# Message stage of a graph network: counts turned as bf16 in runs of eight blocks, one pass for the bias row, TensorE's steps written out

## What is computed

```python
# layer 0: relational convolution
Hb = jnp.einsum('ni,bio->bno', h, V)                  # 4 bases
m = sum_b w_comp[etype][:, b] * Hb[b][src]; m = m * norm
agg = jax.ops.segment_sum(m, dst)
hn = jax.nn.relu(agg + h @ loop_w + bias)
y = hn @ ffn_w.T + ffn_b + h                          # then layer norm with ln_g, ln_b
# layer 1: two transformer convolutions, 2 heads, over the same edges
alpha = jnp.sum(q[dst] * k[src], axis=-1) / np.sqrt(C)
ex = jnp.exp(alpha - segment_max(alpha)[dst])
out = segment_sum(v[src] * ex / segment_sum(ex)[dst]) + x @ Ws + bs
```

## Time and profile before

| what | before |
|---|---|
| median of 3 runs | 2248.89 us |
| the profiled execution, its own time | 2249.5 us |
| its span | 2247.5 us |
| mean granted TensorE clock | 0.981 |
| busy: TensorE, its weight loads | 94%, 76% |
| busy: VectorE, ScalarE, GpSimd | 71%, 57%, 37% |

### The profile page before, as it was taken

One profiled execution on the slowest core, in us unless ns is written; L12 is line 12 of the kernel. 1 busy time (PEld: TensorE's weight loads), 2 busy tenths in 40 slices (PEclk: granted clock), 3 DMA queues, 4 the chain that ended last, 5 costly groups with the idle time before them and its releaser, 6 DMA issues. The chain is left out here.

```text
span 2247.5 us, 55086 instructions
## 1 busy us (share of the span) xinstructions
PE 2104.2 (94%) x19640; PEld 1707.9 (76%) x19640; DVE 1590.5 (71%) x4061; ACT 1291.7 (57%) x2303; POOL 821.2 (37%) x1091
## 2 busy tenths in 40 slices
PE   1299999999999999999997999999999999999998
PEld 1288888898888888888985677777776677777776
DVE  1458887888888888878873666666664666666765
ACT  1156666665666666666663555556564455565555
POOL 0766776777677667767710000000000000000000
PEclk9599999999999999999998999999999999999999
DMA  4001111111111111111112222222221122222220
GB/s 122 14 31 45 42 46 51 44 45 52 47 38 46 51 48 41 46 51 44 43 40 100 87 78 72 80 85 85 85 85 48 71 94 92 92 92 92 92 92 7
DMA packets 52538, 141.57 MB, mean 63 GB/s; under 512 B 9261, under 2 KB 43755, under 8 KB 45855
## 3 DMA queue, kind: packets, MB, share of 16 engines
q1 hardware_dynamic: 49804, 129.55, 16.3%
q0 software_dynamic: 2576, 9.68, 1.5%
HBM read 93.95 MB, written 45.27 MB: 62 GB/s over the span
## 5 line engine op out<-in xcount | busy, mean ns | idle before, releaser
L778 PE MATMUL ps<-matrixT,x_rows 125*128 125x256 f32 (+1 forms) x2500 | 582.7, 384 | 2.9 <-ACT aggT L864 2.1
L778 PEld LDWEIGHTS ps<-matrixT,x_rows 125*128 125x128 f32 x2500 | 461.4, 191 | 70.9 <-issue 3.3
L845 ACT COPY matrixT<-ps 125x500 f32<-125x500 f32 (+2 forms) x800 | 395.8, 583 | 201.5 <-PE ps L766 197.3
L1468 ACT COPY weightsT_l<-ps 125x500 f32<-125x500 f32 (+1 forms) x450 | 233.8, 542 | 369.2 <-PE ps L1389 369.2
L766 PE MATMUL ps<-high_weights,low_onehot 64*125 64x125 f32 x6300 | 403.8, 279 | 23.2 <-issue 11.3
L1546 DVE CUSTOM_DVE_ANT_0 scores_l<-ps,bias_rows_l 125x500 f32<-125x500 f32 (+1 forms) x700 | 396.8, 619 | 35.3 <-issue 33.7
L766 PEld LDWEIGHTS ps<-high_weights,low_onehot 64*125 64x125 f32 x6300 | 366.2, 189 | 54.0 <-issue 37.2
L1389 PEld LDWEIGHTS ps<-eye,scores_l 125*125 125x125 f32 x2500 | 301.1, 189 | 115.6 <-issue 97.2
L1389 PE MATMUL ps<-eye,scores_l 125*125 125x125 f32 x2500 | 364.2, 286 | 4.8 <-ACT scores_l L1450 3.4
L1554 DVE COPY weightsT_l<-ps 125x500 f32<-125x500 f32 (+1 forms) x250 | 150.0, 600 | 267.3 <-PE ps L1389 264.9
L1450 ACT ACTIVATE scores_l<-scores_l,neg_max_l 125x1500 f32<-125x1500 f32 x200 | 320.9, 1605 | 20.5 <-DVE neg_max_l L1583 20.4
(11 more groups left out here) (154 smaller groups left out, 1864.5 us busy)
## 6 DMA issues: line engine op xcount, KB each, us to landing
bias_rows_l<-bias SPq DMA_DIRECT2D x50, 1562.5 KB, 6.7
bias<-bias SPq DMA_DIRECT2D x150, 250.0 KB
edges<-rec POOLq DMA_DIRECT2D x1, 2014.2 KB, 11.8
x_rows<-in_x SPq DMA_DIRECT2D x1, 1562.5 KB
bias<-bias SPq DMA_DIRECT2D x25, 62.5 KB
x<-x_rows SPq DMA_DIRECT2D x25, 62.5 KB
x_rows_l<-x SPq DMA_DIRECT2D x25, 62.5 KB
out<-rows_l SPq DMA_DIRECT2D x25, 62.5 KB
```

The lines of the kernel that those rows point to most:

```text
L778: last = nc.tensor.matmul(psG[:, BASES * SPLIT * side:BASES * (SPLIT * side + SIDE[side])], x[:, h, :], MT[side][:, 0:SIDE[side], BASES * ...
L845: last = nc.scalar.copy(MT[side][:, at:at + 2 * c - 1:2, 0:COLS], psP[bank][0:R, :].rearrange("p (i c) -> p i c", c=128)[:, 0:c, 0:COLS])
L1468: nc.scalar.copy(PT[i % 8][:, 0:cw[c]], psT[i % 2][0:R, 0:cw[c]]).then_inc(z["pa_ok"], 1)
```

## The change

1. `countsT` becomes bf16, and so does the identity that turns it (`eye16`). The bank psT is seen as 8 blocks of 128 bf16 columns (`psC`). The 25 blocks are turned in four runs of 8, 8, 8 and 1 (`runs`), at TensorE's periods 1, 3, 5 and 6 (`RUN_AT`), where there were seven groups in periods 1 to 7.
2. `logs` takes one run (1000 columns, 125 for the last) per instruction; there are 4 per tile in place of 7. `turn_counts` now waits for `ln_ok`, the logarithm of the run before.
3. `bias_row` is one instruction that reads the logarithm alone: min(ln x 1e28, ln). For a count of 0 the logarithm is about -85 and the result about -8.5e29, for 1 it is 0, for more it is ln. The semaphore `masked` goes. The stores to HBM are 4 per tile in place of 7.
4. TensorE's code is written out for all 25 tiles (`pipeline_loop(pe, step, AFTER, T)`), so that it has no hardware loop in this stage; the other engines keep theirs.
5. `turn_codes` on TensorE and its copies on ScalarE move from period 4 to period 5.
6. In period 7 ScalarE's last piece of `counts_out` goes ahead of the copy into `xT`.

```diff
-        CT = sb("countsT", [R, T, R], F32)
+        CT = sb("countsT", [R, T, R], BF16)
+        eye16 = sb("eye16", [128, 128], BF16)
-        lns = [sb(f"ln{i}", [R, CW], F32) for i in range(2)]
-        bias = [sb(f"bias{i}", [128, CW], F32) for i in range(2)]
+        lns = [sb(f"ln{i}", [R, RUN * R], F32) for i in range(2)]
+        bias = [sb(f"bias{i}", [128, RUN * R], F32) for i in range(2)]
...
+        psC = psT[:, :].bitcast(BF16).rearrange("p (h n) -> p h n", n=128)
...
-                V.tensor_scalar(row, psT[0:R, 0:cw[j]], 0.0, NEG, ALU.is_equal, ALU.mult).then_inc(masked, 1)
-                v.wait_ge(masked, n + 1)
-                V.tensor_tensor(row, row, lns[at][:, 0:cw[j]], ALU.add).then_inc(bias_ok, 1)
+                ln = lns[at][:, 0:cols]
+                V.scalar_tensor_tensor(bias[at][0:R, 0:cols], ln, FAR, ln, ALU.mult, ALU.min).then_inc(bias_ok, 1)
...
-                    if k >= 2 and inside(u):
-                        bias_row(u, par, k - 2)
+                    if k - 1 in RUN_AT and inside(u):
+                        bias_row(u, RUN_AT[k - 1])
...
-                if j % 2 == 0:
-                    pe.wait_ge(ctA_ok, u * PIECES + (j // 2 + 1))
-                    pe.wait_ge(ctB_ok, u * PIECES + (j // 2 + 1))
-                if not is_int(u) or n >= 1:
-                    pe.wait_ge(masked, n)
-                for i in range(cw[j] // R):
-                    last = nc.tensor.transpose(psT[0:R, R * i:R * (i + 1)], CT[:, 4 * j + i, :], eye[0:R, 0:R])
+                n, (g, k) = u * PIECES + i, runs[i]
+                pe.wait_ge(ctA_ok, n + 1)
+                pe.wait_ge(ctB_ok, n + 1)
+                if n >= 1:
+                    pe.wait_ge(ln_ok, n)
+                for h in range(g, g + k):
+                    last = nc.tensor.transpose(psC[0:R, h - g, 0:R], CT[:, h, :], eye16[0:R, 0:R])
...
-                    if k == 4 and inside(w + 1):
+                    if k == 5 and inside(w + 1):
                         turn_codes(w + 1, par)
...
-            pipeline_loop(pe, step, AFTER, LEAD)
+            pipeline_loop(pe, step, AFTER, T)
...
-                nc.scalar.activation(lns[at][:, 0:cw[j]], psT[0:R, 0:cw[j]], ACT.Ln, bias=tiny[0:R, :]).then_inc(ln_ok, 1)
+                nc.scalar.activation(lns[at][:, 0:k * R].rearrange("p (h n) -> p h n", n=R), psC[0:R, 0:k, 0:R], ACT.Ln,
+                                     bias=tiny[0:R, :]).then_inc(ln_ok, 1)
...
                     if k == 7 and inside(z):
-                        nc.scalar.copy(xT[:, bass.ds(z * R, R)], psM[:, 384:384 + R]).then_inc(x_t_ok, 1)
+                        act.wait_ge(x_ps, z + 1)
                     if k >= 5 and inside(w):
                         counts_out(w, 0, k - 5)
+                    if k == 7 and inside(z):
+                        nc.scalar.copy(xT[:, bass.ds(z * R, R)], psM[:, 384:384 + R]).then_inc(x_t_ok, 1)
```

More of the change, by code:

```diff
@@ L39 @@
 PIECES = 4
+RUN = 8
+RUN_AT = {1: 0, 3: 1, 5: 2, 6: 3}
+FAR = 1.0e28
 PARTS = (0, 6, 12, 18, T)
@@ L441, in message @@
         SIDE = (SPLIT, R - SPLIT)
-        cw = widths()
+        runs = [(RUN * i, min(RUN, T - RUN * i)) for i in range(PIECES)]
         node = [sb(f"node{i}", [128, 1], F32) for i in range(2)]
@@ L594, in _, with store @@
             sp.wait_ge(const, 2)
[L596 to L601, removed]
+            def store(u, i):
+                at, (g, k) = i % 2, runs[i]
+                sp.wait_ge(bias_ok, u * PIECES + i + 1)
+                sp.dma_start(m["bias"][bass.ds(u, 1), :, g * R:(g + k) * R].rearrange("a p n -> (a p) n"),
+                             bias[at][:, 0:k * R]).then_inc(out_ok[at], 16)
             def step(t, par):
-                if inside(t - 5):
-                    store(t - 5, 1 - par, CH - 1)
                 if inside(t - 4):
-                    for j in range(CH - 1):
-                        store(t - 4, par, j)
+                    for i in range(PIECES):
+                        store(t - 4, i)
                 if inside(t - 5):
@@ L612, in _ @@
             pipeline_loop(sp, step, AFTER, LEAD)
-            sp.wait_ge(out_ok[0], 16 * ((T * CH + 1) // 2))
-            sp.wait_ge(out_ok[1], 16 * (T * CH // 2))
+            for at in range(2):
+                sp.wait_ge(out_ok[at], 16 * (T * PIECES // 2))
             sp.wait_ge(kept[0], 16 * ((T + 1) // 2))
@@ L802, in step @@
                         sums(w, 0, k - 4)
-                    if k >= 1 and inside(u):
-                        turn_counts(u, k - 1)
+                    if k in RUN_AT and inside(u):
+                        turn_counts(u, RUN_AT[k])
                     if k == 4 and inside(u):
@@ L852, in counts_out @@
                 if side == 0 and (not is_int(s) or s >= 1):
-                    act.wait_ge(c_ps, s * CH - CH + min(2 * piece + 2, CH))
+                    act.wait_ge(c_ps, s * PIECES - PIECES + piece + 1)
                 act.wait_ge(evac_ok, s * PERIODS + PERIODS // 2 * (side + 1))
@@ L865, in sums_out, with logs @@
                                psG[:, BASES * lo:BASES * (lo + n)].rearrange("p (n b) -> p b n", b=BASES)).then_inc(aggT_ok, 1)
-            def logs(u, par, j):
-                n, at = u * CH + j, (par + j) % 2
+            def logs(u, i):
+                n, at, k = u * PIECES + i, i % 2, runs[i][1]
                 act.wait_ge(c_ps, n + 1)
@@ L894, in step @@
                         counts_out(u, 1, 3)
[L895 to L899 removed]
+                    if k in RUN_AT and inside(u):
+                        logs(u, RUN_AT[k])
+                    if k == 5 and inside(w + 1):
                         act.wait_ge(codes_ps, w + 2)
@@ L1063, in pipeline_loop @@
         step(t, t % 2)
-    with eng.Fori(0, (T - lead) // 2) as k:
-        step(k * 2 + lead, lead % 2)
-        step(k * 2 + lead + 1, (lead + 1) % 2)
+    if lead < T:
+        with eng.Fori(0, (T - lead) // 2) as k:
+            step(k * 2 + lead, lead % 2)
+            step(k * 2 + lead + 1, (lead + 1) % 2)
     for t in range(T, T + after):
```

22 lines of the change are left out of this document (8 added, 14 removed).

## The result

The changed kernel takes 2196.37 us (median of 4 runs, 2195.24 to 2196.52); the kernel before took 2248.39 us in runs on the same chip. The ratio is 0.9766, with a 95% interval of 0.9749 to 0.9783: 52 us less. The forecast was 2203 us, with a range of 2194 to 2233. The profiled execution took 2196.48 us with a span of 2194.5, where before it was 2247.5.

What follows compares the result with a forecast made beforehand. The prediction took TensorE's instruction stream to bound the steady message stage. Transposes 31.2, loop 11.3, codes 3.9 and drain 2.5, less 2 for ScalarE, gave 46.9 us off 2249.5: 2203 us, range 2194 to 2233 including rivals A and B.

Steps and rivals of the forecast that it cites:

- The size of a transpose: TensorE's 625 count transposes: bf16 takes each from 0.110 to 0.060 us, 31.2 us saved.
- Rival A: Count transposes: the weight load does not shrink in bf16, so 3 us saved in place of 31; 2231 us, chance 0.27.
- The group's length adds nothing: TensorE's groups of count transposes: longer groups gain nothing, as the products behind them are on the same engine.
- Only TensorE has no room: Steady message stage: TensorE busy 1056.6 of 1075.0 us, the other engines less, so time follows TensorE's instruction stream.
- Codes a period later: TensorE's wait for GpSimd's coefficients at `turn_codes`: moving it a period later removes the whole 3.9 us, with no new wait.
- Bias row, worth nothing in the steady stage: VectorE's bias row: 4.6 in place of 9.3 us per tile, but VectorE waits for TensorE, so no steady-stage gain.
- TensorE written out: TensorE's steady stage: writing out the steps removes the 8 loop returns, 11.3 us saved.
- Rival B: TensorE's written-out code is fetched too slowly, paying back the loop's gain in "issue" waits; 2214 to 2218 us, chance 0.08.
- The -2 us for ScalarE: ScalarE's order in period 5 and at the step's end is tight: 2 us of cost for the whole stage.
- Rival C: ScalarE becomes the bound, paying double for two-byte copies and logarithms, slower than before; 2289 us, chance 0.05.
- Drain, 2.5 us: End of the message stage: shorter waits for the bias row, 4.3 us in 4 waits before, save 2.5 us.
- D: The change is not felt, because TensorE's time is set elsewhere; 2247 to 2249 us, chance 0.02.

Runs made afterwards that it cites:

- b_pad128: Kernel before with its f32 count blocks padded to 128 columns, giving a shorter weight load: 2251.15 us, ratio 1.0006.
- b_bf16: Kernel before with only the counts, the identity and the PSUM blocks in bf16, all else as it was: 2244.34 us, ratio 0.9984.
- b_bf16_codes5: Kernel before with bf16 counts and the codes' transposition moved from period 4 to 5: 2214.69 us, ratio 0.9842.
- a_loop: Changed kernel with TensorE's hardware loop put back: 2201.78 us, ratio 0.9796.
- a_busy2: Changed kernel with two extra unused copies of 625 columns on ScalarE in period 5, ahead of its copy of the codes: 2201.64 us, ratio 0.9786.
- a_conv16: Changed kernel with both convolutions' softmax weights in bf16, multiplied by values split into high and low bf16 parts: 2031.24 us, ratio 0.9031.
- b_onepass: Kernel before with only the bias row made in one instruction from the logarithm: 2232.39 us, ratio 0.9932.

## Why the prediction was right in its total and wrong in its parts

- **The size of a transpose** was right: 0.0575 us against the 0.060 taken, 0.110 - 0.0575 = 0.0525 us less, x 625 = 32.8 us against 31.2. Rival A is refuted by the load of 138 ns and, independently, by b_pad128, where a load shortened by as much moved the distance by 0.001 us: the load was not the limit.
- **That the load follows the clock** holds, but was read from the wrong rows. The 327 ns of the earlier trace rows belong to a load of 128 columns, to be set against the 140 ns of line 830 and not the 189, and the profile records no lower clock at that time. What shows it is line 753: 223 ns a load at a granted clock of 0.50 (85 to 91 us), 136 ns in the steady stage.
- **"The group's length adds nothing"** was not quite so. From the start of a group of four to the small product behind it 0.434 us pass on average, but 0.528 where pair products stand behind it; in b_bf16 0.228 and 0.322. The 0.094 us between is paid three times a step before and twice after. With it the groups of a step fall from 2.99 to 1.62 us: 1.37 us, which is the fall of TensorE's own step (43.24 to 41.87).
- **"Only TensorE has no room"** is the step that failed. It was read from busy shares and from the sizes of the waits. Both are true and neither shows how far away the next limit is: a ring through three engines, none of them full but TensorE, already held every looped step without a return, 0.4 us above TensorE's own time. Its only trace was the small wait of the earlier trace rows, 3.9 us in 11 pieces. Here a small wait that recurred in half the steps was the mark of a second limit as long as the first. For the whole change the forecast came out all the same, because two other parts of it, the one pass and the later codes, each loosened a ring that the prediction did not know of: as far as the 32 us of the transposes go, that was luck.
- **"Codes a period later", 3.9 us.** Alone it measured 6.6 us. Its real value is that it sets free the 32 us of the transposes: b_bf16 gave 4 us, b_bf16_codes5 35.5.
- **"Bias row, worth nothing in the steady stage".** Alone 15.6 us, 11.3 of them in the 22 steps. The cover that the prediction named, TensorE's own step, does hide VectorE's busy time, but not the delay of what stands behind the passes in VectorE's queue: line 697's `y`, and with it the ring, and something at the loop's return (gaps of 0.6 us on average in place of 1.4). No run takes the one pass out of the changed kernel, so its price there is not known.
- **"TensorE written out", 11.3 us.** Alone 11. With the one pass already in, only about 5 (a_loop). The prediction added two terms that draw on the same time. Rival B is refuted: no wait for "issue" stands anywhere in the steady stage of the kernel after.
- **The -2 us for ScalarE** were not seen in the changed kernel: no wait from 120 to 1135 us in the list. Rival C is refuted, since cast and logarithm are paid by the element (1108 and 1095 ns). That period 5 has more room than forecast, a_busy2 shows.
- **Drain, 2.5 us.** Outside the 22 steps 7.4 us were gained. The transposes of the three tiles that lie there make 3 x 1.37 = 4.1 us of it. The other 3.3 us are as much as the fall of the bias waits from 4.3 to 1.0, but the waits of the drain fell by 1.7 us in all, so about half of it has no cause that is shown.
- **The sum.** Alone the four parts measured 3.6, 11.1, 15.6 and 6.6 us, together 37 us; the change measured 52. Two errors met, and they pull against each other. The prediction knew nothing of the ring, which holds back the transposes' gain when they stand alone and which the change loosens twice over; and the one pass and the written-out loop overlap. After the change only the stream is left, with 41.87 us a step, and a forecast by the stream (41.9 to 42.0) comes out right then. D is refuted by the result. Had the change been the transposes alone, the same argument would have forecast 2218 us and missed by 26.
- **Term by term,** the span fell by 53.0 us against a sum of 46.9. The transposes with what stands behind them gave 25 x 1.37 = 34.3 (31.2 taken). The waits gave 45.6 - 22 x 1.37 = 15.4 (15.2 taken), so the 2 us that the prediction's lower end allowed for their shadows were not there. ScalarE's -2 did not come, and 3.3 us are left around the 22 steps (2.5 taken).

## What to carry to other kernels

Before a cut in the busiest engine is priced, follow each recurring small wait back through the engines until it returns to where it began, and add up that ring: where it is about as long as the step, the cut alone is worth the difference of the two and no more. Look at the steps one by one, too: where two kinds alternate, each may have its own limit. Work on an idle engine still costs what it delays behind it in its queue. Price edits together, along the ring and along the stream, and take the later one each time; moving a reader a period later was a cheap way to loosen this ring.

## What the runs showed of the hardware

- The weight load does not set the pace of transposes: blocks of 125 columns come 0.108 us apart in f32 with a load of 189 ns, 0.107 with one of 141, and 0.0575 in bf16 with one of 138.
- The short f32 load of 128 columns (140 ns, line 830) was seen with transposes only: the f32 products of line 778 load 128 columns in 190 ns.
- A bf16 weight load takes 138 to 139 ns for 125 columns and 109 to 112 ns for 64 (a_conv16), so some 0.46 ns for each further column, against 189 and 136 ns and 0.87 ns a column in f32. The Trainium skill ("TensorE: Matmul & The Clock Gate", section LDWEIGHTS) gives columns / 1.2 ns, with no term for the type, 104 ns here; both kinds measured differ from it and from each other, and the measurement decides.
- GpSimd's time for one and the same instruction varies by near a factor of two: in b_bf16, line 552 below takes 1.69 or 1.90 us, and 1.06 us at other times; the fold behind it 0.73 or 1.36. Three such groups at the longer time are 4.8 us each where the first took 3.7. VectorE was busy during the whole of each run of line 552 that took 1.9 us, and for 44% of the time of those that took 1.06. But less work on VectorE did not shorten the ring's part on GpSimd, root to last coefficient: 28.2 us on average before and in b_onepass, 28.9 in b_bf16, 28.8 in the changed kernel. What decides the time of one is not shown.

GpSimd in order of time, kernel b_bf16:

```profile
584.41 0.73 POOL L553 TENSOR_TENSOR coef_parts<-coef_parts 128x256 f32<-128x256 f32 x1
...
586.47 1.90 POOL L552 TENSOR_TENSOR coef_parts<-kinds,comp 128x512 f32<-128x512 f32 x1
588.44 1.36 POOL L553 TENSOR_TENSOR coef_parts<-coef_parts 128x256 f32<-128x256 f32 x1
```

- A return of TensorE's hardware loop left it idle for 0.5 to 1.5 us, by what surrounds it; with the steps written out that idle time is gone. What sets its length stays open.
